# Last attention layer: query maxima from whole numbers in 48 rows, two key halves on the upper and lower array rows at once

## The chip, the cores and the metric

The kernel runs on one core of one Trainium2 chip. The metric is the device time of one execution in microseconds (us), median over several executions. Before the change it is 1283.31 us over 3 executions (1281.79 to 1284.55).

## The reference

Four decoder layers, each a cross attention and a feed-forward part with routing. Only the attention of the last layer is changed. Queries, keys and values are rounded to 8-bit steps with a scale of their own (`_fq_sym`), and so are the softmax weights (`_fq_unsigned`), for which the kernel needs each query row's largest score before it takes exponentials.

```python
B, N, C = x.shape                      # 8, 128, 256: 1024 queries; 1024 keys
q = (x @ Wq + bq).reshape(1, B * N, 16, 16)
kv = (cond @ Wkv + bkv).reshape(1, -1, 2, 16, 16)
k, v = (kv[:, :, 0], kv[:, :, 1])
q = transpose(q * 0.25, (0, 2, 1, 3)) ; k = transpose(k, ...) ; v = transpose(v, ...)
q = _fq_sym(q, axis=-1)                # s = max|q| / 127 per head and query; round(q / s) * s
k = _fq_sym(k, axis=-1)
v = _fq_sym(v, axis=2)
attn = softmax(einsum('bhqd,bhkd->bhqk', q, k), axis=-1)
attn = _fq_unsigned(attn, axis=-1)     # s = max(attn) / 255
out = einsum('bhqk,bhkd->bhqd', attn, v)
return out.reshape(B, N, C) @ Wp + bp
```

## The kernel before, in words

One function `plan()` writes a list of steps; each engine then walks the whole list in the same order and does its own part of each step. The engines meet by semaphores only, so an engine that waits in one step holds back its later steps. For each attention layer `merge` sorts several streams of steps by a due time counted in units; the due times stand by hand in `TIMES`.

The last layer (`ATT[3]`) works in 4 units of 256 queries (2 tiles of 128) against all 1024 keys, 16 heads of depth 16. A unit consists of:

- **front**: `fn` (normalise and transpose two x tiles), `fq3` (project them, result into `tmp`), `quant` (VectorE's function `quantise`: maximum, step, reciprocal, scale, round with MAGIC, times the step; result in `tmp2`), `fqt` (TensorE transposes `tmp2`, ScalarE copies it to `qf`), `split` (GpSimd cuts the fp32 values into three bf16 parts in `sq`), `store` (SyncE's queue, `sq` to the scratch `scr_q` in DRAM) and `packs` (three DMAs from there into the rows of `QP`). Six blocks of 16 rows hold the products high*high, high*middle and so on, so that a contraction over 96 rows gives a full-precision score. The keys went the same way into `KP` in the feed-forward stage before (`k3load`, 8 steps, three DMAs each, between the tiles of that stage).
- **maxima** (`smax`, two parts of 32 tiles each): TensorE multiplies 128 queries of a head by 512 keys (96 rows) into one bank of `psB` (line 1210), VectorE takes the maximum along the row (line 1770). `psB` has 3 banks in a ring (`BANKS`), which all short products share (`take("M")` and `take("S")` count on the same ring); a tile waits until the bank's last user has been read.
- **negmax** per part: VectorE cuts the negated maxima into three bf16 parts (lines 1784 to 1801), TensorE transposes them, ScalarE copies them to `nmT`, and three small DMAs (line 1050) put them as rows 96 to 98 beside the queries, against rows of ones in `KP`.
- **body** (36 steps, lag 3): `st` (line 1244: four products of 99 rows, 4 heads x 256 queries, into one half of `psT`; ScalarE's exponential, line 1545), `round` (GpSimd, line 2149), `pv` (line 1278 four fp16 products of 32 columns, line 1288 four fp32 products of 32 columns for the row sums), `onorm` at the end of each group of heads.
- **finish**: `ot`, `oy`, next statistics.

A unit's maxima are merged with the second half of the body of the unit before and the first half of its own; between two `st` of the body stand two `smax` tiles. The first unit's first part has no body beside it. The front of unit u+1 stands where the maxima of unit u begin. At the very start, the GpSimd queue holds the split of unit 0 ahead of the last four gathers of the feed-forward stage (`gather2` of batches 6 and 7), and VectorE needs these for the tiles that follow. `w12load` (ScalarE's queue, line 1587, 3 MB) fetches the first expert's weights of the last feed-forward part, during the body of unit 1.

## Time and profile before

| | |
|---|---|
| median of 3 executions | 1283.31 us |
| profiled execution: its own time | 1287.61 us |
| its span in the profile | 1285.7 us |
| TensorE busy | 969.9 us (75%) |
| VectorE busy | 650.2 us (51%) |
| ScalarE busy | 439.9 us (34%) |
| GpSimd busy | 383.9 us (30%) |
| first `smax` product of the layer to the last one | 813.9 to 1061.9 us |
| mean of one `smax` product, of one maximum | 434 ns, 685 ns |

The span is one execution under the profiler and is longer than the median of the unprofiled ones. PE is TensorE's matmuls, PEld its weight loads, DVE VectorE, ACT ScalarE, POOL GpSimd, SP SyncE. A matmul's own duration includes its way through the array, so rows of neighbouring matmuls overlap; the difference of their starts is what they cost. PEclk is the granted TensorE clock as a share of 2.4 GHz.

### The profile page before, as it was taken

What the parts mean: (1) busy time and instruction counts of PE and PEld (TensorE: products, weight loads), DVE (VectorE), ACT (ScalarE), POOL (GpSimd) and SP (SyncE); (2) the same over time, 40 slices, a digit from 0 to 9 for tenths busy, and PEclk for the clock granted to TensorE, in tenths of its full rate; (3) what the DMA queues carried; (4) which work ended last, traced back from release to release, by engine and by line L of the source; (5) the groups of instructions that cost most, each with busy time, mean ns of one, the idle gap of its engine ahead of it and who ended that gap; (6) DMA issues with size and microseconds to landing.
All of it is one profiled execution on the core that took longest, in us unless ns stands there. A gap on an engine that the chain in (4) does not pass through costs nothing.

```text
span 1285.7 us, 18945 instructions
## 1 busy us (share of the span) xinstructions
PE 969.9 (75%) x6616; PEld 574.1 (45%) x6616; DVE 650.2 (51%) x1546; ACT 439.9 (34%) x720; POOL 383.9 (30%) x527
## 2 busy tenths in 40 slices
PE   1868787688448889677637981698989999469993
PEld 1434444577314435455424761234444544336662
DVE  1757663335258723256764335787878783301111
ACT  1335545211015521144410430045655667112210
POOL 3213210211375200333304006135555557110002
PEclk9989989688759989878858995569989999679997
DMA  8643641365454200455432663201031000620002
GB/s 191 137 98 90 171 104 62 145 205 170 150 130 123 64 25 0 131 84 98 82 131 77 199 183 94 45 1 38 2 104 35 2 2 2 268 88 25 17 13 74
DMA packets 117820, 117.64 MB, mean 91 GB/s; under 512 B 71848, under 2 KB 107240, under 8 KB 114408
## 3 DMA queue, kind: packets, MB, share of 16 engines
q1 hardware_dynamic: 106496, 95.58, 27.3%
q10 hardware_dynamic: 8160, 12.46, 3.4%
q0 software_dynamic: 3072, 8.39, 2.2%
q8 instruction: 56, 0.92, 0.3%
q14 instruction: 36, 0.29, 0.1%
HBM read 90.53 MB, written 29.62 MB: 93 GB/s over the span
## 4 chain that ended last, share of the span: by engine, by line
PE 48%; DVE 14%; POOL 6%; issue 6%; DMA 4%; ACT 3%; SPq 0%; POOLq 0%; ACTq 0%; DVEq 0%
PE psT L1392 6%; PE psT L1093 6%; PE psB L1093 5%; PE psT L1244 5%; PE psB L1210 4%; PE psO L1288 3%; DVE mxp L1770 3%; PE psB L1406 3%; PE psT L1355 2%; PE psB L1433 2%; PE psB L1457 2%; PE psO L1278 2%; PE psB L1101 1%; POOL scr_sorted L2161 1%; DVE mxp L1774 1%
## 5 line engine op out<-in xcount | busy, mean ns | idle before, releaser
L1770 DVE TENSOR_REDUCE mxp<-psB 128x1 f32<-128x512 f32 x256 | 162.4, 685 | 41.6 <-PE psB L1210 40.5
L1244 PE MATMUL psT<-whole 99*128 99x256 bf16 (+2 forms) x1024 | 156.9, 279 | 11.3 <-issue 10.9
L1774 DVE TENSOR_REDUCE mxp<-psB 128x2 f32<-128x512 f32 x192 | 122.6, 685 | 52.5 <-PE psB L1216 52.4
L1216 PE MATMUL psB<-whole 96*128 96x256 bf16 x384 | 77.8, 315 | 64.3 <-issue 55.0
L1244 PEld LDWEIGHTS psT<-whole 99*128 99x128 bf16 (+2 forms) x1024 | 98.5, 103 | 60.8 <-issue 27.8
L1545 ACT ACTIVATE Pt<-psT,ln 128x1024 f32<-128x1024 f32 x96 | 106.6, 1114 | 54.9 <-PE psT L1244 53.8
L1545 ACT ACTIVATE Pt<-psT 128x1024 f32<-128x1024 f32 x96 | 97.9, 1023 | 73.2 <-PE psT L1244 71.5
L2096 POOL TENSOR_TENSOR rstd<-vare,cst 128x1 f32<-128x1 f32 x64 | 35.6, 559 | 277.8 <-DVE vare L1694 277.6
L1210 PE MATMUL psB<-whole 96*128 96x512 bf16 x256 | 96.6, 434 | 4.2 <-DVE mxp L1770 3.0
L1216 PEld LDWEIGHTS psB<-whole 96*128 96x128 bf16 x384 | 31.4, 107 | 114.2 <-issue 84.4
L1392 PE MATMUL psT<-whole,qf 128*128 x176 | 81.4, 606 | 0.6 <-ACT qf L1594 0.6
L1101 PE MATMUL psB<-cst,xn 128*128 128x128 f32 x96 | 23.3, 333 | 76.6 <-DVE xn L1634 76.5
L2149 POOL TENSOR_SCALAR nb_t<-Pt 128x1024 f16<-128x1024 f32 x64 | 66.9, 1045 | 40.6 <-ACT Pt L1545 38.6
L1276 PE MATMUL psO<-Pt,whole 128*32 128x256 f32 x768 | 65.6, 416 | 3.4 <-ACT Pt L1545 2.5
L2022 DVE TENSOR_TENSOR Pt<-psT,Pt 128x512 f32<-128x512 f32 x22 | 15.2, 692 | 99.3 <-ACT Pt L1600 99.3
L1093 PE MATMUL psT<-xn_t,whole 128*128 128x512 f32 (+1 forms) x128 | 59.3, 624 | 0.7 <-ACT xn_t L1490 0.7
L1288 PE MATMUL psO<-Pt,cst 128*32 128x256 f32 x768 | 59.8, 389 | 0.0
L1490 ACT ACTIVATE xn_t<-psB 128x256 f32<-128x256 f32 x48 | 18.2, 380 | 114.5 <-PE psB L1101 114.5
L1101 PEld LDWEIGHTS psB<-cst,xn 128*128 128x128 f32 x96 | 11.0, 159 | 91.1 <-issue 83.3
L1210 PEld LDWEIGHTS psB<-whole 96*128 96x128 bf16 x256 | 19.6, 101 | 69.7 <-issue 38.8
L2180 POOL DMA_INDIRECT xn_t<-scr_sorted_out,idx x8 | 7.6, 950 | 139.5 <-DMA scr_sorted_out<-xn 137.4
L1392 PEld LDWEIGHTS psT<-whole,qf 128*128 128x128 f32 x176 | 32.5, 195 | 33.9 <-issue 33.9
(300 smaller groups left out, 1793.7 us busy)
## 6 DMA issues: line engine op xcount, KB each, us to landing
whole<-in_w SPq DMA_DIRECT2D x32, 512.0 KB, 4.9
whole<-in_w SPq DMA_DIRECT2D x5, 3072.0 KB, 10.2
xn<-scr_sorted ACTq DMA_DIRECT2D x42, 128.0 KB, 2.2
scr_q<-sq SPq DMA_DIRECT2D x48, 96.0 KB, 1.9
scr_k<-sk SPq DMA_DIRECT2D x48, 96.0 KB, 1.9
whole<-scr_k SPq DMA_DIRECT2D x24, 192.0 KB, 3.5
whole<-scr_k SPq DMA_DIRECT2D x72, 64.0 KB, 3.8
whole<-scr_q SPq DMA_DIRECT2D x64, 64.0 KB
```

Source lines behind the costliest of these rows:

```text
L1093: ins = pe.matmul(dst, lhsT=lhs(kd), rhs=rhs(kd), start=(kd == 0), stop=(kd == halves - 1))
L1101: ins = pe.transpose(dst[:, kd * P:(kd + 1) * P], xn[:, xs.b, kd * P:(kd + 1) * P], ident)
L1210: ins = pe.matmul(dst, lhsT=q_at[:, h * A.T + s.tc * P:h * A.T + (s.tc + 1) * P], rhs=k_at[:, h * NT + half * 512:h * NT + (half + 1) * 51 ...
L1216: ins = pe.matmul(dst[:, i * 256:(i + 1) * 256], lhsT=q_at[:, h * A.T + s.tc * P:h * A.T + (s.tc + 1) * P], rhs=k_at[:, h * A.T:(h + 1) * ...
L1244: ins = pe.matmul(psT[:, s.n % 2, i * A.T:(i + 1) * A.T], lhsT=k_at[:, h * kw + s.c * P:h * kw + (s.c + 1) * P], rhs=q_at[:, h * A.T:(h + ...
L1276: ins = pe.matmul(dst, lhsT=VA[:, u.g % 3, s.c * A.H + h, :], rhs=pr, start=first, stop=last)
L1288: ins = pe.matmul(dst, lhsT=const("sumsel"), rhs=pr, start=False, stop=last)
L1392: ins = pe.matmul(psT[:, s.n % 2, k * 512:(k + 1) * 512], lhsT=xeT[:, s.i % 2, kd, :], rhs=whole[:, bass.ds(s.un.k * SLOTW + at, 512)], st ...
L1545: act.activation(p_slot(A, s.p)[:, 0:4 * A.T], psT[:, s.n % 2, 0:4 * A.T], ACT.Exp, bias=bias).then_inc(T_used[s.n % 2], 1)
L1770: dve.tensor_reduce(mxp[:, s.un.g % 2, at:at + 1], psB[:, s.n % BANKS, :], AX.X, ALU.max).then_inc(bank_used[s.n % BANKS], 1)
L1774: dve.tensor_reduce(mxp[:, s.un.g % 2, at:at + 2], psB[:, s.n % BANKS, :].rearrange("p (h n) -> p h n", h=2), AX.X, ALU.max).then_inc(bank ...
L2149: pool.tensor_scalar(n_slot(s.p)[:, 0:w], p_slot(s.A, s.p)[:, 0:w], 1.0, OFFSET, ALU.mult, ALU.add).then_inc(rounded, 1)
```

## The change

The integer queries (after rounding, before the multiplication by the step) are exact in one bf16 part. Their products with the three parts of the keys need 48 rows only. A new pair of steps `fit` transposes and copies them (`ints_of`, in `sk`), `ints` stores them to DRAM (one DMA), and `ints_packs` brings them back with six DMAs into `QI`: three copies at rows 0 to 47, three at rows 64 to 111. The keys are laid out anew in `KP`: three parts at rows 0 to 47, and again at rows 64 to 111, with the high part in rows 48 to 63 between them; seven blocks of 16 rows in place of six. `QP` follows with seven blocks in four DMAs, and the body's products have 112+3 rows.

One `smax` step now takes one head and tile against 1024 keys: one product in rows 0 to 47 on the first 512 keys, one in rows 64 to 111 on the second 512, into two banks, both of which must be free before the first of them starts. VectorE takes the two maxima as before; the maxima are multiplied by the query's step once per part (a new VectorE instruction in `negsplit`). The wait for `q_packed` moves from the first `smax` to the first `st`. `QI` of units 0 to 2 lies in `w0`, so `w12load` moves from the body of unit 1 to the end of the maxima of unit 2; that of unit 3 lies in `ctx_t`.

```diff
+K3_ROWS = ((0, 0, 3), (48, 0, 1), (64, 0, 3))
+Q3_ROWS = ((0, 0, 3), (48, 2, 1), (64, 1, 2), (96, 1, 1))
...
-                           rows=96, lows=(3 if layer == 3 else 2) if has_max else 0)
+                           rows=112 if layer == 3 else 96, lows=(3 if layer == 3 else 2) if has_max else 0)
...
-    dict(front=0.077, fronts=[0.0, 0.01, 0.02, 0.03, 0.04, 0.058, 0.06, 0.079], store=0.294, packs=0.3, max=1.011, ...
+    dict(front=0.077, fronts=[0.0, 0.01, 0.02, 0.03, 0.04, 0.05, 0.054, 0.058, 0.06, 0.079], ints=0.2, ints_packs=0.21, store=0.294, packs=0.3, max=1.011, ...
...
-                out += [fq3(j) for j in range(A.nb)] + [q3, fqt(0), fqt(1), split]
+                out += [fq3(j) for j in range(A.nb)] + [q3, fit(0), fit(1), fqt(0), fqt(1), split]
...
-            per = A.H * A.NC * P // 512 // A.parts
+            per = (A.H if A.layer == 3 else A.H * A.NC * P // 512) // A.parts
...
-                            r.last_S = add("smax", A=A, un=r, tc=tc, j=j, first=(tc == 0 and j == 0), n=take("S")).n
+                            s = add("smax", A=A, un=r, tc=tc, j=j, first=(tc == 0 and j == 0), n=take("S"))
+                            s.n2 = take("S") if A.layer == 3 else None
+                            r.last_S = s.n2 if A.layer == 3 else s.n
...
-            if A.layer == 3 and u == 1:
-                streams += [([lambda: add("w12load", s=last["td"])], u + at["body"] + 0.5, u + at["body"] + 0.5)]
+            if A.layer == 3:
+                streams += [([lambda r=units[u]: add("ints", un=r)], u + at["ints"], u + at["ints"]),
+                            ([lambda r=units[u]: add("ints_packs", un=r)], u + at["ints_packs"], u + at["ints_packs"])]
+            if A.layer == 3 and u == 2:
+                streams += [([lambda: add("w12load", s=units[2].last_S)], u + at["max_end"] + 0.05, u + at["max_end"] + 0.05)]
...
+                elif s.kind == "ints":
+                    u = s.un
+                    for m in u.m_ints:
+                        turn(sp, bank_used, m)
+                    if u.u >= 2:
+                        sp.wait_ge(ints_packed[u.g % 2], 96 * (u.u // 2))
+                    sp.dma_start(di[u.g % 2].rearrange("(m p) n -> p m n", m=2), ints_of(u.g)).then_inc(ints_stored[u.g % 2], 16)
+                elif s.kind == "ints_packs":
+                    u = s.un
+                    sp.wait_ge(ints_stored[u.g % 2], 16 * (u.u // 2 + 1))
+                    for r in (0, 64):
+                        for c in range(3):
+                            at = r + 16 * c
+                            sp.dma_start(QI(u.u)[at:at + 16, :].rearrange("d (h n) -> d h n", h=16),
+                                         di[u.g % 2].rearrange("(d h) n -> d h n", d=16)).then_inc(ints_packed[u.g % 2], 16)
...
+                elif s.kind == "fit":
+                    dst = m_begin(s.m)
+                    pe.wait_ge(ints_made, s.i + 1)
+                    for j in range(s.un.A.nb):
+                        ins = pe.transpose(dst[:, j * P:(j + 1) * P], tmp[:, j * 256 + s.c * P:j * 256 + (s.c + 1) * P], ident)
                     ins.then_inc(bank_ready[s.m % BANKS], 1)
...
-                    if s.first:
+                    if s.first and A.layer == 3:
+                        pe.wait_ge(ints_packed[u.g % 2], 96 * (u.u // 2 + 1))
+                        pe.wait_ge(k3_in, 48 * len(K3_AT))
+                    elif s.first:
...
-                        h, half = s.j // 2, s.j % 2
-                        ins = pe.matmul(dst, lhsT=q_at[:, h * A.T + s.tc * P:h * A.T + (s.tc + 1) * P],
-                                        rhs=k_at[:, h * NT + half * 512:h * NT + (half + 1) * 512],
-                                        start=True, stop=True)
+                        free(pe, bank_used, s.n2)
+                        for r, n in ((0, s.n), (64, s.n2)):
+                            keys = s.j * NT + (512 if r else 0)
+                            ins = pe.matmul(psB[:, n % BANKS, :],
+                                            lhsT=QI(u.u)[r:r + 48, s.j * A.T + s.tc * P:s.j * A.T + (s.tc + 1) * P],
+                                            rhs=KP[r:r + 48, keys:keys + 512], start=True, stop=True)
+                            ins.then_inc(bank_ready[n % BANKS], 1)
...
+                elif s.kind == "fit":
+                    ...
+                    act.activation(ints_of(u.g)[:, s.c, :], m_slot(s.m), ACT.Copy).then_inc(bank_used[s.m % BANKS], 1)
...
-                link(dve.tensor_scalar(dst, dst, MAGIC, MAGIC, ALU.add, ALU.subtract))
+                link(dve.tensor_scalar(src, dst, MAGIC, MAGIC, ALU.add, ALU.subtract))
+                dve.sem_inc(ints_made, 1)
...
+                        link(dve.tensor_tensor(mx.rearrange("p (t h) -> p t h", t=A.TC),
+                                               mx.rearrange("p (t h) -> p t h", t=A.TC), step, ALU.mult))
...
+def pack3(sp, dst, src, width, sem, blocks, h0, h1):
+    for at, c0, n in blocks:
+        sp.dma_start(dst[at:at + n * 16, :].rearrange("r (h n) -> r h n", h=16)[:, h0:h1, :],
+                     src[c0:c0 + n, :, 0:width].rearrange("c (d h) n -> (c d) h n", d=16)[:, h0:h1, :]).then_inc(sem, 16)
```

## Rows read from the trace of the kernel before

**Rows 1.** The page's costliest groups: busy us, mean ns of one, idle before, releaser

```profile
L1770 DVE TENSOR_REDUCE mxp<-psB 128x1 f32<-128x512 f32 x256 | 162.4, 685 | 41.6 <-PE psB L1210 40.5
...
L1210 PE MATMUL psB<-whole 96*128 96x512 bf16 x256 | 96.6, 434 | 4.2 <-DVE mxp L1770 3.0
```

**Rows 2.** Stretches of the layer: length, busy time per engine, PEclk, DMA share, GB/s

```profile
822.00:844.00 22.00, 20.74 (x37) 3.65 (x36) 21.82 (x41) 0.37 (x1) 3.11 (x4) 0.50 0.25 54
...
880.00:920.00 40.00, 38.93 (x401) 17.33 (x399) 32.73 (x59) 24.38 (x27) 23.60 (x24) 0.97 0.14 31
```

**Rows 3.** Timeline of one body step at full clock: start, duration, instruction

```profile
897.09 0.29 PE L1278 MATMUL psO<-whole 128*32 128x256 f16 x4
...
897.21 0.61 PE L1288 MATMUL psO<-Pt,cst 128*32 128x256 f32 x8
897.25 1.11 ACT L1545 ACTIVATE Pt<-psT,ln 128x1024 f32<-128x1024 f32 x1 [0.52 <-PE psT L1244]
...
897.75 0.61 PE L1210 MATMUL psB<-whole 96*128 96x512 bf16 x2
...
898.17 1.29 DVE L1770 TENSOR_REDUCE mxp<-psB 128x1 f32<-128x512 f32 x2 [0.34 <-PE psB L1210]
898.19 0.60 PE L1244 MATMUL psT<-whole 99*128 99x256 bf16 x4
...
898.72 0.29 PE L1278 MATMUL psO<-nb_t,whole 128*32 128x256 f16 x4
```

**Rows 4.** Waits between 855 and 1063 us: total, times, longest

```profile
DVE mxp L1770 <- PE psB L1210: 38.2, 67, 2.6
```

**Rows 5.** Timeline of a pair of maxima products at half clock, the next `st`

```profile
854.50 1.00 PE L1210 MATMUL psB<-whole 96*128 96x512 bf16 x2
...
855.33 0.61 PE L1244 MATMUL psT<-whole 99*128 99x256 bf16 x4
```

**Rows 6.** Chain that ended last, unit 0's first maxima to the first body step

```profile
821.31 18.04 DVE mxp L1770 x30
...
840.22 0.17 DVE npt L1801
...
847.24 0.85 PE psT L1244 x4
```

**Rows 7.** Timeline: a product at half clock and the maximum behind it

```profile
880.00 0.63 PE L1210 MATMUL psB<-whole 96*128 96x512 bf16 x1
...
880.67 0.69 DVE L1770 TENSOR_REDUCE mxp<-psB 128x1 f32<-128x512 f32 x1 [1.05 <-PE psB L1210]
```

**Rows 8.** Chain that ended last, front of unit 1

```profile
818.85 0.77 DVE tmp L1657 x2
819.76 1.09 PE psB L1145 x4
```

**Rows 9.** Timeline and chain between the split of unit 0 and the first maxima

```profile
798.71 1.25 SPq L2207 DMA_DIRECT2D whole<-scr_q  x3
...
799.97 6.81 DMA ctx_t<-scr_sorted_out,idx
```

**Rows 10.** The same stretch in steps of 2 us, columns as in rows 2

```profile
794.00:796.00 2.00, 0.00 (x0) 0.00 (x0) 1.86 (x6) 0.00 (x0) 1.80 (x2) 0.50 0.00 0
...
802.00:804.00 2.00, 0.00 (x0) 0.00 (x0) 0.34 (x2) 0.00 (x0) 1.58 (x4) 0.50 0.99 201
```

**Rows 11.** Timeline: small DMAs of units 0 and 2, the `st` that needs the latter

```profile
843.67 2.09 SPq L1050 DMA_DIRECT2D whole<-nmT  x3
...
1006.21 1.98 SPq L1050 DMA_DIRECT2D whole<-nmT  x3
...
1010.67 0.60 PE L1244 MATMUL psT<-whole 99*128 99x256 bf16 x4
```

**Rows 12.** Landing of the 3 MB load of line 1587; chain in the stage before

```profile
DMA to landing us min/median/max: 17.1/17.1/17.1
...
721.40 8.18 DMA scr_sorted_out<-xn
```

More of the change, by code:

```diff
@@ L143 @@
     dict(front=0.498, store=0.58, packs=0.683, body=1.604, end=3.227, start=0.084, span=1.053),
-    dict(front=0.077, fronts=[0.0, 0.01, 0.02, 0.03, 0.04, 0.058, 0.06, 0.079], store=0.294, packs=0.3, max=1.011, max_end=1.919, neg=2.006, body=1.639, end=3.415, start=0, span=1.008, max_first=1.026)]
+    dict(front=0.077, fronts=[0.0, 0.01, 0.02, 0.03, 0.04, 0.05, 0.054, 0.058, 0.06, 0.079], ints=0.2, ints_packs=0.21, store=0.294, packs=0.3, max=1.011, max_end=1.919, neg=2.006, body=1.639, end=3.415, start=0, span=1.008, max_first=1.026)]
 def plan():
@@ L247, in front @@
             r.packed_before = packed[r.g % 2]
-            packed[r.g % 2] += 16 * (6 if A.layer == 1 else 3)
+            packed[r.g % 2] += 16 * (3, 6, 3, len(Q3_ROWS))[A.layer]
             r.packed = packed[r.g % 2]
@@ L291, in fqt, with fit, f @@
                 return f
+            def fit(m):
+                def f():
+                    s = add("fit", un=r, c=m, i=r.i, m=take("M"))
+                    r.m_ints = (r.m_ints or []) + [s.m]
+                return f
             def split():
@@ L590, in sorted_pairs @@
                 add("k3load", i=K3_AT.index(t), m=shared)
-        last["td"] = tiles[TILES2 - 1].s
         def gather(b):
@@ L733, in flamingo @@
         qs = late[:, 304:400].rearrange("p (k h) -> p k h", k=3)
+        kept = late[:, 432:496].rearrange("p (r h) -> p r h", r=2)
         w_at2 = sb("w_at2", [P, 4, 2, 256])
@@ L797, in flamingo @@
         dk = [nc.dram_tensor(f"scr_k{i}", [3, 2 * P, 256], BF16).ap() for i in range(2)]
+        di = [nc.dram_tensor(f"scr_i{i}", [2 * P, 256], BF16).ap() for i in range(2)]
         dk3 = nc.dram_tensor("scr_k3", [3, 2 * P, NT], BF16).ap()
@@ L850, in flamingo @@
         quant_q = sem("quant_q")
+        ints_made = sem("ints_made")
+        ints_stored, ints_packed = pair("ints_stored"), pair("ints_packed")
         v_quant = sem("v_quant")
@@ L930, in wait_packs, with ints_of, QI @@
                 pe.wait_ge(k_packed[g % 2], s.un.packed)
-            else:
-                pe.wait_ge(k3_in, 48 * len(K3_AT))
+        def ints_of(g):
+            return sk[:, g % 2, 0, :].rearrange("p (m n) -> p m n", m=2)
+        def QI(u):
+            return w0[:, 2048 * u:2048 * (u + 1)].bitcast(BF16) if u < 3 else \
+                ctx_t[:, :, :].rearrange("p k n -> p (k n)").bitcast(BF16)
         block = ctx.enter_context(nc.Block())
@@ L1035, in _ @@
                     sp.wait_ge(q_stored[u.g % 2], 32 * (u.g // 2 + 1))
-                    pack(sp, A, QP[:, u.g % 3, :], scratch(dq, A, u.g), A.T, q_packed[u.g % 2], is_q=True)
+                    if A.layer == 3:
+                        pack3(sp, QP[:, u.g % 3, :], scratch(dq, A, u.g), A.T, q_packed[u.g % 2], Q3_ROWS, 0, 16)
+                    else:
+                        pack(sp, A, QP[:, u.g % 3, :], scratch(dq, A, u.g), A.T, q_packed[u.g % 2], is_q=True)
                     if u.k is not None:
@@ L1236, in _ @@
                             pe.wait_ge(k_ones, 16 * {0: 3, 1: 6, 3: 10}[A.layer])
-                        else:
+                        if A.layer >= 2:
                             wait_packs(pe, s)
@@ L1638, in bc, with quantise @@
                 return ap.to_broadcast(shape)
-            def quantise(src, dst, H, n):
+            def quantise(src, dst, H, n, step):
                 s4 = src.rearrange("p (j d h) -> p j h d", j=n, h=H)
@@ L1644, in quantise @@
                 link(dve.tensor_reduce(scale, s4, AX.X, ALU.max, apply_absolute_value=True))
-                link(dve.tensor_scalar(qs[:, 1, 0:n * H], qs[:, 0, 0:n * H], 1.0 / 127.0, 1e-8, ALU.mult, ALU.max))
-                link(dve.reciprocal(qs[:, 2, 0:n * H], qs[:, 1, 0:n * H]))
+                link(dve.tensor_scalar(step, qs[:, 0, 0:n * H], 1.0 / 127.0, 1e-8, ALU.mult, ALU.max))
+                link(dve.reciprocal(qs[:, 2, 0:n * H], step))
                 for j in range(n):
@@ L1732, in _ @@
                         link(dve.tensor_scalar(tmp[:, 0:w], tmp[:, 0:w], 0.25, None, ALU.mult))
-                    quantise(tmp[:, 0:w], tmp2[:, 0:w], 16, s.un.A.nb)
+                    quantise(tmp[:, 0:w], tmp2[:, 0:w], 16, s.un.A.nb, kept[:, s.un.g % 2, :] if s.s else qs[:, 1, 0:32])
                 elif s.kind == "vscale":
@@ L2206, in pack @@
         else:
-            sp.dma_start(rows[:, h0:h1, :], src[c0:c0 + n, :, 0:width].rearrange("c (d h) n -> (c d) h n", d=A.d)[:, h0:h1, :]
+            sp.dma_start(rows, src[c0:c0 + n, :, 0:width].rearrange("c (d h) n -> (c d) h n", d=A.d)
                          ).then_inc(sem, 16)
```

27 lines of the change are left out of this document (19 added, 8 removed).

## The prediction

> **What bounds the kernel now.** I read the page first, then the stretches of the last attention layer, then the timeline of single steps, and last the chain of waits that ended last. On the page the reader is to see that the maxima wait for TensorE and hardly the other way round: VectorE stood idle 41.6 us before its 256 maxima, 40.5 of them for line 1210, while the 256 products waited 4.2 us [rows 1]. The stretches say the same for the middle of the layer: TensorE is busy 38.93 of 40 us, VectorE 32.73, ScalarE 24.38 [rows 2]. The other stretch is the opposite case: unit 0's first maxima, with no body beside them, keep VectorE busy 21.82 of 22 us at half TensorE clock [rows 2].
>
> One body step at full clock takes 897.09 to 898.72, that is 1.63 us [rows 3]: 0.12 for the four fp16 products, 0.54 for the row sums, 0.44 for the two maxima products (897.75 to 898.19), 0.53 for `st`. VectorE needs 1.29 of that and idles 0.34, ScalarE needs 1.11 and idles 0.52. So TensorE's issue order sets the pace here, and any time taken from the pair of maxima products shortens the step, down to some 1.3 us where VectorE would take over.
>
> The starts hold a second thing. Four products of 256 columns at 2.4 GHz are 0.43 us of columns, yet `st` takes 0.53 before the 32-column products begin, and the row sums (also 0.43 of columns) 0.54 before the 128-column ones; the maxima products, 1024 columns or 0.43 us, take 0.44 before `st`, which has the same shape of array. So a change of the array's division costs 0.10 to 0.11, and staying in one costs 0.01 [rows 3]. At half clock, where these columns are 0.85 us, the maxima products take 0.83 before `st`: nothing for staying either [rows 5].
>
> **The change, part by part.** All terms are of the profiled execution: 1287.61 us, of which the span is 1285.7 and 1.9 lie around it; the median of the runs is 4.3 below. I carry the difference over to the median.
>
> *The pair.* Four 32-column products with 1024 columns together take 0.12 us [rows 3], so column strips do run together. Row strips no row shows. From below: two at once, 512 columns, 0.21 plus 0.01; from above: one after the other, 0.44. I take together, since the strips of the other direction do.
> *The new change of division.* A product in 48 rows leaves the 128-row arrangement, and the `st` behind it returns. From below it costs 0.01 (the maxima products to `st` now), from above 0.11 (both changes above). I take 0.11, the row that it is nearest to, and 0.01 more for the second weight load. The pair then costs 0.22 + 0.11 + 0.01 = 0.34 where 0.44 stood: 0.10 gained per step. With the lower bound it is 0.21; if the two don't overlap, the step loses 0.11.
>
> The Trainium skill, page "TensorEngine Tiling (Array Packing)", section "Key Properties", says that tiles operate independently but that changing the tiling mode, not just the tile, drains the TensorE. The trace agrees for column strips, with 0.10 to 0.11 us a change; no row of before has row strips. The same page gives 2x for a contraction of 64 or less; by that alone the pair would gain 0.21 a step, twice what I count.
>
> How many steps: VectorE waited 67 times for a maxima product between 855 and 1063 us [rows 4]. Some five of these stand in the fronts, where something else is late; I count 62. 62 x 0.10 = 6.2 us. At half clock (847 to 855) four steps give up 0.83 and get 0.43 + 0.11 + 0.01: 4 x 0.28 = 1.1. Gained: 7.3 (bounds 14.9 and -6.8). In the rest of the layer VectorE or nothing of the pair is late.
>
> *Two banks at a time.* There are three banks. A pair can't start before the first maximum of the pair before is taken, where until now a product could start three maxima ahead. At full clock that hides: 0.69 for the maximum, 0.04 for the wait, some 0.42 for a product from start to VectorE [rows 3] make 1.15, less than two maxima (18.04 / 30 = 0.60 each, 1.20 a pair) [rows 6]. At half clock the product takes 0.67 [rows 7]: 0.69 + 0.04 + 0.67 = 1.40, against 1.20. Unit 0's first part runs at half clock, 15 such pairs: 15 x 0.20 = 3.0 lost. Behind it the small DMAs of the first part and six pairs end together, as now (840.4 to 847.24 [rows 6]; at the new pace 2.1 until the third pair is issued, 1.2 for it, the transposes and the copy, 3.6 for the DMAs: 6.9 us), so nothing more. Bounds: 0, if the clock should rise there, and 5.
>
> *The fronts.* The transposes of the integers (four more of line 1145's kind) start 0.77 earlier than those of the scaled values, but last 1.09 at half clock [rows 8], and both now stand ahead of the second pair. Unit 1: one more maximum ahead of `quantise`, 0.6, and the third maximum starts some 2.2 us after its end (0.3 of the first four outside the head start, 1.09 for the other four, 0.1 for the last bank's copy, 0.67 for a product) instead of 821.31 - 819.62 = 1.7 [rows 6, 8]: 1.1 us. Units 2 and 3: `fqt` needs banks that two maxima after `quantise` must free, 0.5 each. Together 2.1, bounds 1 and 4. The ScalarE copies lie under TensorE's next transposes.
>
> *The new VectorE product in negsplit*: 0.17 to 0.2 (as line 1801, [rows 6]) eight times, half of it where VectorE is late: 0.8.
>
> *DMAs at the start.* The 16 DMA engines idle at 794 to 796 and are full at 802 to 804 (0.99) [rows 10]; the chain goes through the last gather, 6.81 us, beside the three query packs [rows 9]. The integers' store and six packs (896 KB) are issued on SP's queue ahead of the query store, mostly into the idle stretch; the query packs carry 128 KB more, and the split on GpSimd, ahead of four gathers, begins about 0.5 later, behind two more copies. At 0.2 MB/us [rows 10] 0.6 + 0.5 and a remainder of the integers' overlap: 1.5, bounds 0.5 and 4. For units 1 to 3 nobody waits for these: their maxima stand almost a unit later. SP holds nothing urgent behind them; the small DMAs of line 1050 come half a unit later.
>
> *Keys in seven blocks.* Half a megabyte more in the stage before. The chain there waits once on such traffic (8.18 us [rows 12]): one sixth of a load, 0.4.
>
> *w12load.* It moves next to the small DMAs of unit 2's second part, issued at 1006.21 and needed at 1010.67 [rows 11]. In unit 0 it is 3.6 from the first issue to the `st` behind them (843.67 to 847.24 [rows 6, 11]), here 4.46, so there is about 1 us of slack, and the 3 MB load, which took 17.1 to land [rows 12], is in the same 16 engines. Price 0.7, bounds 0 and 4. ScalarE only issues it; the weights themselves are wanted after 1100, so they are hidden.
>
> *Nothing*: 115 in place of 99 rows (columns count), the later `q_packed` wait (that DMA lands long before the first `st`), stage and lengths of `st`.
>
> Sum: lost 3.0 + 2.1 + 0.8 + 1.5 + 0.4 + 0.7 = 8.5; gained 7.3; +1.2. Profiled 1288.8, median 1284.5: inside what a measurement of this kernel can't tell from no change (0.2%, 2.6 us).
>
> **Rivals.**
> (1) *The forecast*, the change of division is paid: 1284.5; with its terms at their bounds 1280 to 1290.
> (2) *Row strips cost no change of division.* For: staying with 128 columns wide weights costs 0.01 now. Against: every change that the trace has costs 0.10. Gain 62 x 0.21 + 4 x 0.4 = 14.6, less 8.5: -6.1, 1277.2. It decides for faster as soon as a change costs under about 0.05.
> (3) *The halves don't run together.* Each step then has 0.43 + 0.11: 62 x 0.11 + 0.6 lost, plus 8.5: +16, 1299. Against it: column strips overlap fully.
> (4) *Transfers*: the first unit's gathers or the small DMAs behind `w12load` come at their upper bounds: 2.5 + 3.3 more, half of each: +4, about 1287.5. For: 0.99 DMA share, 1 us of slack.
>
> **Numbers.** Chances: (1) 0.45, (2) 0.28, (3) 0.12, (4) 0.15. Of (1) I give 0.27 to no difference, 0.13 to slower, 0.05 to faster, since the small losses are more likely more than fewer; (2) 0.26 faster, 0.02 same; (3) slower; (4) 0.12 slower, 0.03 same. Faster 0.31, same 0.32, slower 0.37. The range takes in (2) and (4) and leaves out (3) and tails: 1275.5 to 1290.5; the forecast's own is 1281 to 1289.
>
> **What would show it.** In the timeline of a full-clock step: the two products of the pair start within 0.05 of each other and `st` starts 0.33 after them (0.22 for (2), 0.55 for (3)); the step is 1.53. Line 1770's run of 30 in unit 0 becomes some 21 us with an idle 0.2 before each pair. The first maxima product starts about 1.5 later than 813.9. The `st` that follows the small DMAs of unit 2 shows a DMA as releaser if (4) holds. The forecast is wrong if the clock of that first stretch is full, or if the pair's cost isn't 0.34.

## The result, and the profile after

The changed kernel takes 1298.31 us (median of 4 executions, 1297.09 to 1308.25), the kernel before beside it 1283.93 (4 executions). The ratio is 1.0117, 95% interval 1.0076 to 1.0158: slower by 1.2%, where 1284.5 and "no difference" were forecast, and outside the range of 1275.5 to 1290.5. The profiled execution took 1298.73 us, its span is 1296.9.

The steady step came out as forecast. Timelines of TensorE and VectorE at full clock in the changed kernel; columns as in [rows 3], lines 1262, 1297, 1331, 1341 and 1831/1834 are the earlier 1210, 1244, 1278, 1288 and 1770:

```profile
888.84 0.39 PE L1262 MATMUL psB<-whole 48*128 48x512 bf16 x2
889.16 0.61 PE L1297 MATMUL psT<-whole 115*128 115x256 bf16 x4
889.71 0.29 PE L1331 MATMUL psO<-whole 128*32 128x256 f16 x4
889.83 0.61 PE L1341 MATMUL psO<-Pt,cst 128*32 128x256 f32 x8
890.36 0.39 PE L1262 MATMUL psB<-whole 48*128 48x512 bf16 x2
...
889.27 0.69 DVE L1831 TENSOR_REDUCE mxp<-psB 128x1 f32<-128x512 f32 x1 [0.23 <-PE psB L1262]
889.87 0.68 DVE L1834 TENSOR_REDUCE mxp<-psB 128x1 f32<-128x512 f32 x1
```

The pair holds TensorE for 0.32 us (888.84 to 889.16) where 0.44 stood [rows 3], the step is 1.52 instead of 1.63. So the halves run together and the change of division is paid. The loss is elsewhere. The page's groups of the two maxima lines and of the pairs, and the waits between 820 and 1075 us (total, times, longest):

```profile
L1831 DVE TENSOR_REDUCE mxp<-psB 128x1 f32<-128x512 f32 x128 | 88.5, 691 | 49.5 <-PE psB L1262 48.7
L1834 DVE TENSOR_REDUCE mxp<-psB 128x1 f32<-128x512 f32 x128 | 87.2, 681 | 0.0
L1262 PE MATMUL psB<-whole 48*128 48x512 bf16 x192 | 45.3, 463 | 25.4 <-DVE mxp L1831 20.8
```

```profile
DVE mxp L1831 <- PE psB L1262: 45.8, 94, 3.4
PE psB L1262 <- DVE mxp L1831: 18.3, 24, 1.9
PEld psB L1262 <- DVE mxp L1834: 15.9, 12, 1.3
PE psB L1262 <- DVE mxp L1834: 5.7, 7, 1.1
```

In [rows 1] TensorE stood idle 4.2 us before the products in all, 3.0 of it for line 1770; now it is 25.4 before three quarters of the pairs alone, 20.8 of it for line 1831, and VectorE still waits more for products than before (48.7 against 40.5). Each side waits for the other: that points to a ring of buffers too short for what is taken from it at once, not to an engine that is too slow. Nineteen waits, 12 of the weight loads and 7 of the products, are for line 1834, the *second* maximum of the pair before, which the forecast had never counted with.

Where it happens is seen in one of the three stretches between two bodies. TensorE in the changed kernel:

```profile
906.03 0.39 PE L1262 MATMUL psB<-whole 48*128 48x512 bf16 x2 [1.24 <-DVE mxp L1831]
...
908.42 0.28 PE L1279 MATMUL psB<-ident,npt 128*24 128x128 bf16 x2
909.41 0.39 PE L1262 MATMUL psB<-whole 48*128 48x512 bf16 x2 [0.71 <-DVE mxp L1834]
...
912.50 0.41 PE L1348 MATMUL psB<-cst,Oe 128*128 128x128 f32 x2 [0.20 <-DVE mxp L1834]
913.75 0.39 PE L1262 MATMUL psB<-whole 48*128 48x512 bf16 x2 [0.84 <-DVE mxp L1834]
914.07 0.61 PE L1297 MATMUL psT<-whole 115*128 115x256 bf16 x4
915.00 0.39 PE L1262 MATMUL psB<-whole 48*128 48x512 bf16 x2 [0.31 <-DVE mxp L1831]
915.32 1.04 PE L1297 MATMUL psT<-whole 115*128 115x256 bf16 x4
```

And the same stretch in a second profile of the kernel before:

```profile
901.53 0.39 PE L1210 MATMUL psB<-whole 96*128 96x512 bf16 x1 [0.52 <-DVE mxp L1770]
...
904.03 0.28 PE L1226 MATMUL psB<-ident,npt 128*24 128x128 bf16 x2
904.24 0.87 PE L1210 MATMUL psB<-whole 96*128 96x512 bf16 x2
...
907.56 0.41 PE L1295 MATMUL psB<-cst,Oe 128*128 128x128 f32 x2
908.07 0.39 PE L1210 MATMUL psB<-whole 96*128 96x512 bf16 x1
908.29 0.60 PE L1244 MATMUL psT<-whole 99*128 99x256 bf16 x4
```

The single transposes (the negated maxima at 908.42, the output at 912.50) take one bank of the same ring. After one of them the pair's two banks are those of the two maxima just under way, so it waits for both. Before, the first of two products could go into the one free bank at once. At 915.32 `st` lasts 1.04 instead of 0.61: the granted clock has dropped, from the level of 2.4 GHz to that of 1.2. It does so behind all three stretches; windows of the changed kernel, and of the kernel before over the last two of them (length, busy time of PE, PEld, DVE, ACT, POOL, PEclk, DMA share, GB/s):

```profile
915.00:921.80 6.80, 6.80 (x35) 2.46 (x36) 4.32 (x8) 4.72 (x5) 4.18 (x4) 0.52 0.00 0
987.30:994.10 6.80, 6.80 (x36) 2.40 (x36) 4.26 (x8) 4.62 (x5) 4.05 (x4) 0.52 0.01 2
1055.40:1062.20 6.80, 6.72 (x34) 2.39 (x34) 4.40 (x7) 4.62 (x5) 3.88 (x4) 0.51 0.00 0
```

```profile
941.00:1091.00 150.00, 142.43 (x1575) 70.20 (x1574) 102.86 (x205) 96.67 (x105) 89.82 (x90) 1.00 0.11 33
```

To compare single executions I count from a mark inside each: the first transposes of the last layer, which follow 12 us of idle TensorE in every kernel. Ahead of it executions differ: e4 and e12 below, both with the earlier layers of the kernel before, need 764 and 785 us for them. The two marks and the first maxima product, in the changed kernel and then in the kernel before:

```profile
771.54 0.66 PE L1142 MATMUL psB<-cst,xn 128*128 128x128 f32 x2 [12.00 <-DVE xn L1693]
...
803.75 0.61 PE L1262 MATMUL psB<-whole 48*128 48x512 bf16 x2
```

```profile
774.13 0.66 PE L1101 MATMUL psB<-cst,xn 128*128 128x128 f32 x2 [11.95 <-DVE xn L1634]
...
808.86 1.06 PE L1210 MATMUL psB<-whole 96*128 96x512 bf16 x2
```

All columns below are differences of such starts, in us. A: mark to first maxima product. B: from there to the first `st`. T: the three stretches between bodies, six body steps each. F: the fronts of units 2 and 3, five steps each. W: the three steps around the small DMAs of unit 2's second part. All: mark to the same late step of unit 3's body, behind the last maxima (1087.4 in the changed kernel). The first two lines are two executions of one kernel, so what a line can differ by chance is seen there.

```
kernel                              A      B     T     F     W    All   median  ratio to before (95%)
before                            35.0   32.7  45.2  35.1   5.8  298.5
before, again                     34.7   32.8  45.2  33.9   5.8  295.1  1285.65 1.0023 (0.9995-1.0052)
changed                           32.2   38.8  57.7  36.6  10.2  315.9  1298.31 1.0117 (1.0076-1.0158)
e1  own bank                      31.8   33.7  48.8  37.6  10.2  300.7  1290.13 1.0056 (1.0021-1.0091)
e2  load later                    32.0   38.6  58.1  35.7   5.5  309.3  1296.03 1.0101 (1.0058-1.0143)
e8  e1 and e2                     32.1   33.7  52.0  37.6   5.5  299.5  1284.83 1.0022 (0.9994-1.0049)
e7  112 rows, own bank            32.3   33.6  47.7  36.9  10.2  303.6  1292.26 1.0075 (1.0042-1.0107)
e9  112 rows, two banks           31.9   39.2  52.4  35.9  10.4  312.3  1299.66 1.0087 (1.0059-1.0114)
e6  no integers, two banks        35.7   38.8  55.9  36.7  11.2  318.1  1304.99 1.0189 (1.0134-1.0244)
e10 e8, integers in unit 0 only   31.8   33.5  50.2  36.7   5.5  296.5  1289.24 0.9999 (0.9970-1.0028)
e11 e10, 12 pairs in full rows    32.1   33.7  48.0  36.9   5.5  295.9  1280.21 0.9981 (0.9947-1.0015)
e12 before, load at new place     34.6   32.8  45.2  33.9  10.2  301.9  1289.24 1.0030 (0.9995-1.0066)
```

### The profile page after: what moved, and what is told of

Same layout as the page of the kernel before. It is cut to its first block, busy times and chain, and to the rows that moved or that the text cites. A ratio compares the mean times of both kernels' runs of the same rounds, so it can differ in the third digit from the quotient of the medians.

```text
span 1296.9 us, 19181 instructions
## 1 busy us (share of the span) xinstructions
PE 956.7 (74%) x6632; PEld 561.6 (43%) x6632; DVE 655.4 (51%) x1554; ACT 443.1 (34%) x728; POOL 385.4 (30%) x527
## 4 chain that ended last, share of the span: by engine, by line
PE 50%; DVE 14%; issue 5%; POOL 4%; DMA 4%; ACT 3%; SPq 1%; another core or an unknown queue 1%; POOLq 0%; DVEq 0%; ACTq 0%
PE psT L1134 7%; PE psT L1297 6%; PE psT L1445 6%; PE psB L1134 5%; PE psB L1262 4%; PE psO L1341 3%; PE psB L1459 3%; PE psB L1510 2%; DVE mxp L1831 2%; PE psT L1408 2%; PE psB L1486 2%; PE psO L1331 2%; PE psB L1142 1%; ACT Pt L1604 1%; DVE mxp L1838 1%
## 5 line engine op out<-in xcount | busy, mean ns | idle before, releaser
L1297 PE MATMUL psT<-whole 115*128 115x256 bf16 (+2 forms) x1024 | 160.5, 284 | 13.2 <-issue 9.4
L1604 ACT ACTIVATE Pt<-psT 128x1024 f32<-128x1024 f32 x96 | 98.0, 1024 | 72.1 <-PE psT L1297 70.4
L1297 PEld LDWEIGHTS psT<-whole 115*128 115x128 bf16 (+2 forms) x1024 | 91.3, 103 | 67.5 <-issue 48.7
L1831 DVE TENSOR_REDUCE mxp<-psB 128x1 f32<-128x512 f32 x128 | 88.5, 691 | 49.5 <-PE psB L1262 48.7
L1834 DVE TENSOR_REDUCE mxp<-psB 128x1 f32<-128x512 f32 x128 | 87.2, 681 | 0.0
L1269 PEld LDWEIGHTS psB<-whole 96*128 96x128 bf16 x384 | 30.4, 105 | 114.7 <-issue 83.6
L2089 DVE TENSOR_TENSOR Pt<-psT,Pt 128x512 f32<-128x512 f32 x22 | 15.2, 692 | 100.2 <-ACT Pt L1659 100.2
L1262 PE MATMUL psB<-whole 48*128 48x512 bf16 x192 | 45.3, 463 | 25.4 <-DVE mxp L1831 20.8
L2216 POOL TENSOR_SCALAR whole<-Pt 128x1024 f16<-128x1024 f32 x32 | 33.5, 1047 | 51.8 <-issue 30.6
```

Of the source, the lines that this page charges most:

```text
L1262: ins = pe.matmul(psB[:, n % BANKS, :], lhsT=QI(u.u)[r:r + 48, s.j * A.T + s.tc * P:s.j * A.T + (s.tc + 1) * P], rhs=KP[r:r + 48, keys:key ...
L1269: ins = pe.matmul(dst[:, i * 256:(i + 1) * 256], lhsT=q_at[:, h * A.T + s.tc * P:h * A.T + (s.tc + 1) * P], rhs=k_at[:, h * A.T:(h + 1) * ...
L1297: ins = pe.matmul(psT[:, s.n % 2, i * A.T:(i + 1) * A.T], lhsT=k_at[:, h * kw + s.c * P:h * kw + (s.c + 1) * P], rhs=q_at[:, h * A.T:(h + ...
L1604: act.activation(p_slot(A, s.p)[:, 0:4 * A.T], psT[:, s.n % 2, 0:4 * A.T], ACT.Exp, bias=bias).then_inc(T_used[s.n % 2], 1)
L1831: dve.tensor_reduce(mxp[:, s.un.g % 2, at:at + 1], psB[:, s.n % BANKS, :], AX.X, ALU.max).then_inc(bank_used[s.n % BANKS], 1)
L1834: dve.tensor_reduce(mxp[:, s.un.g % 2, at + 1:at + 2], psB[:, s.n2 % BANKS, :], AX.X, ALU.max).then_inc(bank_used[s.n2 % BANKS], 1)
```

## The experiments

**e1: the second product waits for its bank only when its turn comes.** Everything else as in the changed kernel.

```diff
-                        free(pe, bank_used, s.n2)
                         for r, n in ((0, s.n), (64, s.n2)):
+                            if r:
+                                free(pe, bank_used, s.n2)
```

> The changed kernel, but the second product of a pair waits for its own bank only when its turn comes, and the first starts without it. Theory A (the wait for two banks of three is what costs: VectorE-bound stretches between two bodies, 3 x 3.1 us, the start 3 us, and the half clock that follows them): the runs of maxima go back to 0.60 us each, about 12 us faster than the changed kernel, 1286. Rival B (the strips themselves or the later w12load cost the time): within 2 us of the changed kernel, 1298.

The median falls by 8 us to 1290.13, T from 57.7 to 48.8, B from 38.8 to 33.7. VectorE's maxima of unit 0's first part follow each other every 0.60 us again (817.87, 818.47, 819.07). The two products still run together where both banks are free, so the step of 1.52 stays. One edit gives back over half of the loss, 8.2 of the 14.4 between the medians and 15.2 of the 17.4 to 20.8 in All: the wait is the main cause. The rival falls; 1286 was expected, 4 less than came. The same place in the stretch as above: the first product now goes into the free bank right behind the transposes, as in the kernel before, and the second follows when its bank is free:

```profile
906.04 0.28 PE L1280 MATMUL psB<-ident,npt 128*24 128x128 bf16 x2
906.34 0.39 PE L1263 MATMUL psB<-whole 48*128 48x512 bf16 x1
906.93 0.39 PE L1263 MATMUL psB<-whole 48*128 48x512 bf16 x1 [0.21 <-POOL nb_t L2217]
```

The half clock behind the stretches is gone in this profile (one of them):

```profile
901.70:917.00 15.30, 13.62 (x127) 5.56 (x126) 14.15 (x26) 7.72 (x9) 6.55 (x7) 1.00 0.01 2
```

**e2: the 3 MB load later.** `w12load` at `max_end` + 0.4 instead of + 0.05.

> The changed kernel with the 3 MB load issued a third of a unit later, behind the small DMAs of unit 2's second part. Theory: the st of unit 2's second half no longer waits for them (5.8 us in the chain of the changed kernel), nor the half clock behind it: 4 us faster than the changed kernel, 1294. Rival: the load hits the next small transfers instead, or the wait was for something else: no change, 1298.

W falls from 10.2 to 5.5 and the half clock behind it disappears. The median falls by 2.3, but the intervals of the two ratios overlap, so this rests on the profiles. The changed kernel's `st` there, behind the small DMAs:

```profile
1015.87 0.61 PE L1297 MATMUL psT<-whole 115*128 115x256 bf16 x4 [2.98 <-DMA whole<-nmT]
```

And a window of the changed kernel at the same time; the last two columns are the DMA engines' busy share and GB/s, with the load issued at 1005.60 and the small DMAs at 1008.69:

```profile
1010.50:1016.00 5.50, 2.52 (x34) 0.93 (x27) 3.13 (x5) 2.10 (x2) 2.69 (x3) 1.00 0.72 305
```

**e3: both products in rows 0 to 47.** They then run one after the other; the second half of the maxima uses the same rows of queries and keys, with its own keys.

```diff
-                                            lhsT=QI(u.u)[r:r + 48, ...], rhs=KP[r:r + 48, keys:keys + 512],
+                                            lhsT=QI(u.u)[0:48, ...], rhs=KP[0:48, keys:keys + 512],
```

> The changed kernel with both products of a pair in rows 0 to 47 (same operands' values, no second strip). If the two strips overlap fully, as the 0.32 us from pair to st says, a full-clock step becomes 0.21 longer, 1.73 us, and the kernel some 60 x 0.21 = 13 us slower than the changed one, 1311. If the strips bring nothing, no change, 1298.

The full-clock step was 1.73 as expected: the pair holds TensorE for 0.53.

```profile
903.38 0.60 PE L1262 MATMUL psB<-whole 48*128 48x512 bf16 x2
903.91 0.61 PE L1297 MATMUL psT<-whole 115*128 115x256 bf16 x4
```

But the time was 1358.99, ratio 1.0583 (1.0531 to 1.0634), far over both expectations: TensorE stayed at half clock through long runs of steady steps, without a pause in its work (15.00 busy of 15):

```profile
940.00:955.00 15.00, 15.00 (x92) 4.43 (x92) 5.62 (x10) 5.57 (x5) 5.02 (x5) 0.50 0.00 1
```

**e4: the kernel before with its maxima products in rows 64 to 95 alone.** This leaves out two thirds of each sum, so the maxima are those of a part of the score.

```diff
-                        ins = pe.matmul(dst, lhsT=q_at[:, h * A.T + ...], rhs=k_at[:, h * NT + half * 512:...],
+                        ins = pe.matmul(dst, lhsT=q_at[64:96, h * A.T + ...], rhs=k_at[64:96, h * NT + half * 512:...],
```

> The kernel before, its maxima products in rows 64 to 95 only (high query part times high and middle key part; the rest of the products is left out, so maxima are slightly off). The change of the array's division alone: if it is paid, the st behind the pair starts 0.53 to 0.54 after it instead of 0.44, a step is 1.73 instead of 1.63, the kernel 60 x 0.10 = 6 us slower, 1290. If it is free for row strips, no change, 1284.

It gave 1404.5, ratio 1.0932 (1.0887 to 1.0976). Where it ran at full clock, its step was 1.73, so a change to fewer rows costs 0.10 here too. But it hardly ever did; 60 us of steady steps, fully busy, at half clock:

```profile
890.00:950.00 60.00, 60.00 (x342) 17.86 (x341) 28.73 (x52) 21.38 (x22) 17.80 (x17) 0.50 0.00 1
```

**e5: the kernel before once more**, unchanged.

> The kernel before, unchanged, run as if it were a variant, to see how far one kernel differs from itself. Both theories expect a ratio within 0.3% of 1 and, in the profile, full granted clock through the three stretches between bodies (from about 900 to 1060 us). If these stretches show half clock here too, then the clock drop that the changed kernel shows there is chance and not its doing.

The ratio is 1.0023 (0.9995 to 1.0052), and the second and third stretch between bodies lie in 150 us at full clock (row above). Neither the first profile of this kernel nor e12 has half clock behind any of the three stretches either (T is 45.2 in all three). So the clock drops of the changed kernel there are its own, and a ratio of 1.002 between two variants says nothing.

**e6: no integers, two banks.** No `fit`, no `ints`; `ints_packs` takes the first part of the scaled queries after their store. The maxima are those of rounded queries.

```diff
-                out += [fq3(j) for j in range(A.nb)] + [q3, fit(0), fit(1), fqt(0), fqt(1), split]
+                out += [fq3(j) for j in range(A.nb)] + [q3, fqt(0), fqt(1), split]
...
-                                         di[u.g % 2].rearrange("(d h) n -> d h n", d=16))
+                                         scratch(dq, ATT[3], u.g)[2].rearrange("(d h) n -> d h n", d=16))
```

> The changed kernel without the transposes of the integers, their copies and their store: the pair of 48-row products takes the first part of the scaled queries, whose six packs are sent right ahead of the query packs (so the maxima are those of rounded queries, and negsplit's added operation is a maximum instead of a product, of the same shape). The pair still waits for two banks. Theory A (the loss is the pair's wait for two of three banks in the stretches that VectorE bounds, and the clock that falls behind it): only the fronts come back, about 3 us, so 1295, and half clock still follows the transitions. Rival F (the four added transposes in each front are what delays the stretches between bodies): most of the loss goes, 1288 or less, and no half clock behind the transitions.

It was slower, not faster: 1304.99. Removing four transposes per front hardly moved F (36.7 for 36.6), T fell by 1.8 only, and half clock still followed the second and third stretch, so the rival falls. My own number was off by 10: A is 35.7, against 32.2. The integers' early store gives unit 0's first maxima a head start of 3.5 us, which goes with them, and W is 1 us longer.

**e7 and e9: full rows.** The products are taken of the query parts in all 112 rows, one after the other, while the integers are still prepared. e7 waits for each bank in its turn, e9 for both at first.

```diff
+                        wait_packs(pe, s)                       # first product of a unit
...
-                                            lhsT=QI(u.u)[r:r + 48, ...], rhs=KP[r:r + 48, keys:keys + 512],
+                                            lhsT=q_at[:, ...], rhs=KP[0:112, keys:keys + 512],
```

> The changed kernel with everything that prepares the integers, but the maxima are taken of the full query parts in all 112 rows, one product after the other, each waiting for its own bank only (negsplit's added operation is a maximum instead of a product, of the same shape). It prices all of the change except the pair. Theory A: the step at full clock is 1.63 again (0.11 x 62 = 7 us more than the changed kernel), no starved stretch between bodies (-8 to -11), unit 0's first part back at VectorE's pace (-3): about 1291, that is the kernel before plus some 3 for the fronts and 4 for the load beside unit 2's small DMAs. Rival F (the front work is the loss): 1298 or more, with half clock behind the transitions.

> The variant with full 112-row products one after the other, but the pair waits for both its banks before the first product, as in the changed kernel: the fourth corner beside the changed kernel, its own-bank version and the full-row version, so that the wait is priced without the 48-row products. Theory A (the wait for two banks is what costs, whatever the rows of the products): unit 0's first part grows from 33.6 to some 40 us (at half clock the second product starts 0.4 after the first, so each pair costs 0.2 to 0.4 more than two maxima), the stretches between bodies by 2 to 3 us each: 1302 to 1306, over 8 us above the full-row version. Rival B (the wait costs only where 48-row products also pull the clock down): at most 5 above it, 1297, with full clock behind the transitions.

e7 prices the change without the pair: T 47.7 instead of 45.2, F 36.9 instead of 33.9 to 35.1, W 10.2. With the two-bank wait B grows by 5.6 and T by 4.7, All by 8.7. In unit 0's first part of e9 the pairs stand 1.46 apart (two maxima are 1.20):

```profile
822.72 1.01 PE L1263 MATMUL psB<-whole 112*128 112x512 bf16 x2 [0.45 <-DVE mxp L1832]
824.18 1.01 PE L1263 MATMUL psB<-whole 112*128 112x512 bf16 x2 [0.45 <-DVE mxp L1832]
```

The changed kernel has the same 1.45 (811.26, 812.71, 814.16). So the wait alone does the harm in B. In T, it costs 4.7 with full rows and 8.9 with 48 rows (changed against e1). The medians are 7.4 apart, but the two ran in different batches, and their ratios to the kernel before, 1.0075 and 1.0087, don't separate them; that reading rests on the profiles.

**e8: both repairs**, the edits of e1 and e2.

> The changed kernel with both repairs: the pair's second product waits for its own bank only when its turn comes, and the 3 MB weight load is issued later, behind unit 2's small DMAs. Theory A (the two losses stand in different places and add up): 4 us under the variant with the first repair alone, about 1286, and no half clock at 1009 us. Rival (the load's stretch only uncovers another wait): no gain over 1290.

1284.83, ratio 1.0022 (0.9994 to 1.0049): not told apart from the kernel before. W is 5.5, so the rival falls, although the intervals of e1 and e8 overlap. Half clock still followed the third stretch here (1041 to 1051 us), which alone makes T 52.0 instead of 48.8.

**e10: e8 with integers for unit 0 alone.** Units 1 to 3 take the first part of the scaled queries (rounded queries, approximate maxima); no `fit`, no added product in `negsplit`.

```diff
+                out += ... + [q3] + ([fit(0), fit(1)] if r.u == 0 else []) + [fqt(0), fqt(1), split]
...
+                        if s.un.u == 0:
                             link(dve.tensor_tensor(mx..., mx..., step, ALU.mult))
```

> The variant with both repairs, and the integers are made, stored and packed for unit 0 alone; for units 1 to 3 the pair takes the first part of the scaled queries (a rounded form of them, so these maxima are approximate), without the four transposes in each front and without negsplit's product. It keeps the head start of unit 0's first maxima. Theory A (what is left of the loss are the front's transposes and the product in VectorE's stretches): fronts of units 1 to 3 back by 1.0 to 1.3 us each, transitions by 0.4 to 1.2 each, so 4 us or more under the version with both repairs, about 1280, below the kernel before. Rival (the stretches between bodies are long for another reason): 1284 or more.

Ratio 0.9999 (0.9970 to 1.0028). F falls by 0.9 and each of the first two stretches by 0.2, the product's own duration; the third falls by 1.4, with a shorter drop of the clock. All is 3.0 lower, the 4 us expected were too much; the medians, of different batches, don't show a difference.

**e11: e10, and full rows where VectorE sets the pace.** A pair with no `st` since the pair before (4 in each stretch, 12 of 128) is taken in 112 rows.

```diff
+                        full = u.u > 0 and not since            # `st` appends to since
+                        since.clear()
...
+                                            lhsT=(q_at if full else QI(u.u)[r:r + 48])[:, ...],
+                                            rhs=KP[0:K, ...] if full else KP[r:r + 48, ...],
```

> As the variant whose integers are made for unit 0 alone, but in units 1 to 3 a pair that has no scores product between it and the pair before (four of each stretch between bodies, 12 of 128) is taken in all 112 rows, one product after the other. There VectorE sets the pace, so the longer products cost nothing. Theory A with the clock (fewer array rows at work pull the granted clock down when TensorE also idles): full clock behind all three transitions, each at or under 15.1 to 16.3 us, so 3 us under that variant, ratio to the kernel before about 0.997. Rival (the clock behind the third transition falls for another reason, or the first of these products waits for its turn of banks as before): no gain, ratio 1.000, and half clock at some 1050 us again.

1280.21 beside 1282.89, ratio 0.9981 (0.9947 to 1.0015): the lowest ratio of all, but not told apart from 1 or from e10, so it doesn't decide between the two expectations. The clock did what was expected in this profile, T is 48.0, and the last 150 us of the layer ran in full. But e1 had full clock behind all three stretches too, with 48 rows throughout, so this doesn't show that the full rows did it:

```profile
941.50:1094.50 153.00, 142.98 (x1580) 67.87 (x1572) 103.99 (x213) 97.18 (x107) 89.79 (x90) 1.00 0.18 52
```

**e12: the kernel before with `w12load` at its new place**, one part of the change alone.

```diff
-            if A.layer == 3 and u == 1:
-                streams += [([lambda: add("w12load", s=last["td"])], u + at["body"] + 0.5, u + at["body"] + 0.5)]
+            if A.layer == 3 and u == 2:
+                streams += [([lambda: add("w12load", s=last["td"])], u + at["max_end"] + 0.05, ...)]
```

> The kernel before with one part of the change alone: the 3 MB weight load moves from unit 1's body to the end of unit 2's maxima, where the changed kernel has it. Theory A (its packets hold up the small DMAs that the scores of unit 2's second part wait for, whatever the products are): a wait of some 4 us for the small DMAs near 1010 us, half clock for 3.4 us behind it, and 1287.5 (ratio 1.003). Rival (it only hurts beside the changed kernel's other traffic or its earlier second half): no wait, ratio 1.000.

W is 10.2, 4.4 more, with this wait and half clock for 3.4 us behind it. The ratio, 1.0030 (0.9995 to 1.0066), agrees but could also be 1.

```profile
1018.47 0.61 PE L1244 MATMUL psT<-whole 99*128 99x256 bf16 x4 [2.63 <-DMA whole<-nmT]
```

## Why the prediction was wrong

**The step that failed** is in *Two banks at a time*: "At full clock that hides". It compared one pair with the two maxima before it, with the third bank free: 1.15 against 1.20. Inside the body steps that holds; VectorE idles there and nothing waits. It took the whole layer for such steps. Between two bodies eight to ten maxima fall into one body step, VectorE sets the pace (the state that [rows 2] show in unit 0's first maxima), and transposes take single banks of the ring. There the pair waits for the second maximum, and by the same sum 0.68 for it, 0.04 and 0.42 lie open. T grew by 12.5; 8.9 of that went with e1, and 2.5 of the 3.6 left are there without the pair too (e7). The price had been nothing.

**The clock went with it.** In the last 4 us ahead of the drop at 915.3 TensorE was busy for 2.44; at the same place the kernel before has 3.75 (904.2 to 908.2). Then come 6.8 us at half clock, and so behind each stretch: the lengths of the first step there are 3.09, 2.77 and 2.76 where 1.86, 1.85 and 1.85 stood. I had carried the full clock of [rows 3] over to stretches that I was about to make idle. What part the rows have in it is less certain than the wait: the changed kernel and e2 had a drop behind all three stretches, e6 (the same wait and rows) behind two, e9 (wait, full rows) a short one of 3.4 us behind one, e8 and e10 (48 rows, no wait) behind the third, e1, e7 and e11 none.

**Two banks at half clock** had its mechanism right and its size half: forecast 1.40 a pair and 3.0 in all, measured 1.455, B + 6.0. The pairs' pace gives 15 x 0.255 = 3.8. "So nothing more" behind it was wrong: six more pairs at that pace end B, and e1 takes 5.1 of it back.

**w12load**: priced 0.7 with an upper bound of 4; it costs 4.4, in the kernel before too. The "about 1 us of slack" was set against a price of 0.7 with no row of small DMAs beside such a load; here the engines carried 305 GB/s while they were under way. Rival (4) named it, but at half of its upper bound.

**DMAs at the start**: 1.5 later was forecast, 2.5 to 2.8 earlier was measured (A). `ints_packs` goes ahead of the split, the store and the query packs, and the first maxima no longer wait for these. e6 shows it from the other side. I had read the moved `q_packed` wait as costing nothing, and missed that it gives. (The first product of the kernel before starts at 814.33; the 813.9 on record is its weight load.)

**The pair**: 0.32 for 0.34, rival (3) refuted, rival (2) refuted at full clock. By the Trainium skill, page "TensorEngine Tiling (Array Packing)", section "Key Properties", tiles operate independently and a change of tiling mode drains TensorE; the trace agrees with both: in e3, in the same rows, the pair holds 0.53, which is 0.43 of columns and 0.10 for the change, and in different rows it holds 0.32, so 0.22 is left for the two products. The 2x that the prediction takes from that page is an "up to 2x" there; the pair gained a quarter. But 62 steps were too many. Of 42 steps of 1.63 with two maxima in the kernel before, 37 are 1.52 to 1.56 now, and eight of 1.74 are 1.63: some 5 us, not 6.2. The 1.1 at half clock didn't come: the first two whole steps last 2.69 and 2.66. (The upper bound of 14.9 doesn't come out of its terms; rival (2) has 14.6 from the same.)

**Fronts and negsplit**: 2.1 and 0.8 were forecast. F grew by 1.5 to 2.7 over two fronts, and the product costs 0.2 a stretch. The spread of F is the clock: behind each of the two fronts every kernel of the table has half clock, the kernel before too, for 3.4 or for 6.8 us. Behind the second one in the kernel before again and in the first profile of before:

```profile
937.50:940.70 3.20, 3.20 (x21) 1.67 (x21) 1.05 (x2) 1.60 (x3) 1.41 (x2) 0.50 0.00 0
944.20:950.80 6.60, 6.04 (x39) 2.89 (x39) 3.00 (x6) 2.44 (x4) 3.88 (x5) 0.50 0.00 0
```

Like with like, F grew by 1.8 to 2.0: 33.9 to 35.7 and 35.9 (e2, e9) with 3.4 us twice, 35.1 to 36.9 (e7) with 3.4 and 6.8. Most of that is not the transposes: e6 and e11, which have none in these fronts, have 36.7 and 36.9 beside the 36.9 of e7, and from e8 to e10, both with 6.8 twice, it is 0.9. All of them, with the transposes or without, have steps of 2.42 and 3.80 where 2.04 and 3.36 stood. What they share is that the tiles are taken in twos; no run takes that alone.

**Keys in seven blocks**: the 0.4 lies ahead of the mark, where executions differ by 20 us. No run shows it.

**The sum**, changed against the second profile of before: A -2.5, B +6.0, T +12.5, F +2.7, W +4.4, the rest -2.2 (the pair's gain, less slow first steps), All +20.8; against the first profile +17.4, and the medians are 14.4 apart. That spread is why terms of 1 us can only be read inside a stretch.

What stays open: what part the rows have in the clock, why half clock follows the third stretch in e8 and e10 and not in e1, and how much of T's 8.9 is clock and how much waiting. Rearranging the single transposes so that the ring stays in step with the pairs wasn't tried.

## What to carry to other kernels

When a change takes two buffers of a ring of three at once, look for the places where a single user shifts the ring, and for the stretches where the reader of the buffers, not the writer, sets the pace: the check in the steady step says nothing of them. Let each product wait for its own buffer; where both are free they still run together. And a load that was moved because its memory is now in use belongs to the change: run the kernel before with that move alone.

## What the runs showed of the hardware

TensorE's granted clock stayed at 1.2 GHz while TensorE was busy all the time. With the 512-column products in 48 rows one after the other it was at 0.50 in 15 us of 15.00 busy (e3); in 32 rows, in 60 us of 60.00 busy (e4), although the other products of the step kept their 99 to 128 rows. It didn't fall out of full work: TensorE had idled for part of the 4 us before. But full work didn't bring it back for long. e3 ahead of and in one spell of half clock, behind the first stretch between bodies, then e4, behind the front of unit 2:

```profile
928.50:932.50 4.00, 2.92 (x17) 1.13 (x16) 3.85 (x9) 1.25 (x3) 0.10 (x1) 1.00 0.00 0
932.60:959.70 27.10, 27.10 (x157) 8.53 (x156) 11.68 (x23) 11.85 (x12) 10.52 (x11) 0.50 0.00 1
```

```profile
869.40:873.40 4.00, 1.40 (x20) 0.48 (x18) 3.83 (x8) 1.11 (x1) 1.05 (x1) 1.00 0.00 0
873.50:972.30 98.80, 97.62 (x559) 30.80 (x559) 45.32 (x85) 35.94 (x38) 33.34 (x33) 0.50 0.06 13
```

In the kernel before, e3's place has no half clock, and e4's has 3.4 us of it and then 1.00 again:

```profile
879.30:882.50 3.20, 3.20 (x21) 1.57 (x20) 1.01 (x2) 1.68 (x3) 1.49 (x2) 0.50 0.00 0
883.00:944.00 61.00, 56.74 (x602) 26.78 (x600) 50.46 (x92) 37.60 (x41) 35.12 (x34) 1.00 0.10 21
```

With two products of 48 rows at once the clock held 1.00 over long runs of steps (54 us from 883 in e1), as it did with 96 and 112 rows. The Trainium skill, page "TensorE: Matmul & The Clock Gate", section "The HAM clock gate (the "warmup" mystery)", says that activity releases the throttle. In the rows above, work (almost) without a pause did not release it for 27 and 99 us. The measurement decides here; why it stays down, no run shows. e4 differs from the kernel before only in the rows of one kind of product, 32 instead of 96, in the same order and with the same columns, and its runs of steady steps went from full to half clock. That made both kernels far slower than their steps at full clock explain: 1311 and 1290 us were expected, 1358.99 and 1404.5 measured.
